# Moving the input's transposes behind the output's products in the second half of an attention period

## What is computed

```python
x = x + 0.5 * ffn(layernorm(x))        # ternary weights, exact gelu
x = x + attn(layernorm(x))             # rotary q and k, causal softmax
x = x + 0.5 * ffn(layernorm(x))

def attn(x):
    q, k, v = x @ Wq.T, x @ Wk.T, x @ Wv.T       # each [16, 256, 256], split in 16 heads
    q, k = rope(q), rope(k)
    scores = where(causal, q @ k.T / 4, -inf)
    return softmax(scores) @ v @ Wo.T
```

## Time and profile before

| | us |
|---|---|
| median of 3 runs (lowest, highest) | 606.04 (605.77, 607.61) |
| the profiled execution, its own time | 606.82 |
| its span, first to last instruction | 605.1 |
| PE busy in the span | 567.5 (94%) |
| DVE busy | 458.6 (76%) |
| ACT busy | 345.2 (57%) |
| attention stage, periods with both `XT` and `WO` (p = 1 to 11) | about 205 to 414 of the span |

### The profile page before, as it was taken

How to read it: one execution, slowest core, us unless ns; L and a number is a source line. 1 busy time by engine, 2 the same in 40 slices (tenths; PEclk the granted TensorE clock), 3 DMA queues, 4 the chain that set the end, 5 groups by cost and what they waited for, 6 DMA issues and landing times.

```text
span 605.1 us, 17855 instructions
## 1 busy us (share of the span) xinstructions
PE 567.5 (94%) x6596; PEld 497.1 (82%) x6596; DVE 458.6 (76%) x928; ACT 345.2 (57%) x610; POOL 229.8 (38%) x446
## 2 busy tenths in 40 slices
PE   1899999999689999999999999999878999999997
PEld 1789999999668888888888888888665788899996
DVE  5977777778687988879878798877572777777764
ACT  1765455556236666866667666576556655554542
POOL 6373333333646353542545435434131033333310
PEclk9999999999889999999999999999999999999999
DMA  6630000000867666655575555766500011111111
GB/s 204 213 111 6 0 0 0 0 0 4 242 181 207 184 188 187 166 149 174 165 200 166 149 165 159 206 165 168 153 2 3 1 36 35 35 35 35 35 35 36
DMA packets 71142, 63.45 MB, mean 105 GB/s; under 512 B 4130, under 2 KB 64322, under 8 KB 71106
## 3 DMA queue, kind: packets, MB, share of 16 engines
q1 hardware_dynamic: 69922, 62.81, 35.9%
q10 hardware_dynamic: 1184, 0.14, 0.2%
HBM read 33.03 MB, written 29.36 MB: 103 GB/s over the span
## 4 chain that ended last, share of the span: by engine, by line
PE 82%; DVE 9%; DMA 3%; ACT 2%; POOL 2%; issue 1%; SPq 1%; DVEq 0%; POOLq 0%
PE bank L173 18%; PE bank L534 17%; PE bank L1062 13%; PE bank L670 7%; PE bank L1057 6%; PE bank L1118 5%; PE bank L1193 4%; PE bank L1158 3%; PE bank L156 2%; PE bank L1121 2%; PE bank L1131 2%; DVE mx L860 2%; DVE g_lo L257 1%; DMA w1f<-w1t 1%; PE bank L1181 1%
## 5 line engine op out<-in xcount | busy, mean ns | idle before, releaser
L860 DVE TENSOR_REDUCE mx<-bank 128x2 f32<-128x512 f32 (+1 forms) x192 | 118.4, 681 | 32.8 <-PE bank L1062 32.7
L534 PE MATMUL bank<-w2q,g_hi 128*128 128x256 f32 x512 | 124.4, 284 | 1.8 <-DVE g_lo L257 1.5
L240 ACT ACTIVATE g<-bank,b1c 128x512 f32<-128x512 f32 x128 | 88.1, 691 | 64.7 <-PE bank L173 61.5
L534 PE MATMUL bank<-w2q,g_lo 128*128 128x256 f32 x512 | 122.5, 280 | 0.0
L982 ACT ACTIVATE probs<-bank 128x512 f32<-128x512 f32 x192 | 111.1, 597 | 11.7 <-PE bank L1062 4.1
L534 PEld LDWEIGHTS bank<-w2q,g_hi 128*128 128x128 f32 x512 | 96.4, 188 | 3.6 <-DVE w2q L372 1.3
L534 PEld LDWEIGHTS bank<-w2q,g_lo 128*128 128x128 f32 x512 | 96.4, 188 | 0.6
L312 POOL TENSOR_TENSOR res<-res,b2h 128x1024 f32 (+1 forms) x16 | 38.4, 2400 | 133.2 <-DVE xn L147 128.6
L257 DVE TENSOR_TENSOR g_lo<-g,g_hi 128x512 fp32r<-128x512 f32 x128 | 82.6, 686 | 3.1
L173 PE MATMUL bank<-xt_hi,w1q 128*128 128x512 f32 x240 | 76.9, 402 | 2.0 <-DVE xt_lo L167 2.0
L173 PE MATMUL bank<-xt_lo,w1q 128*128 128x512 f32 x240 | 76.1, 398 | 0.0
(11 more groups left out here) (129 smaller groups left out, 1172.6 us busy)
## 6 DMA issues: line engine op xcount, KB each, us to landing
qk_slots<-parts SPq DMA_DIRECT2D x32, 384.0 KB, 3.7
q<-qk_slots SPq DMA_DIRECT2D x32, 384.0 KB, 4.0
k<-qk_slots SPq DMA_DIRECT2D x32, 384.0 KB, 4.8
qk_slots<-parts SPq DMA_DIRECT2D x32, 256.0 KB, 3.4
res<-x SPq DMA_DIRECT2D x8, 512.0 KB, 3.6
qk_slots<-parts SPq DMA_DIRECT2D x32, 128.0 KB, 3.2
out<-res SPq DMA_DIRECT2D x8, 512.0 KB, 2.9
w1f<-w1t SPq DMA_DIRECT2D x2, 512.0 KB, 6.4
```

The source lines that it names most:

```text
L240: nc.scalar.activation(g[:, f, :], of[:], ACT.Gelu, bias=b1c[:, f:f + 1]).then_inc(g_ready, 1)
L534: last = nc.tensor.matmul(to[:, 0:D], part[:, f, t * P:(t + 1) * P], w2q[:, f, :], start=f == 0 and part is g_hi, stop=f == FC - 1 and par ...
L860: nc.vector.tensor_reduce(o, i, AX.X, ALU.max).then_inc(s_done, 1)
```

## The change

In a second half PE issues the twelve products of `WO` ahead of the four transposes of `XT`, and DVE issues `add_output` ahead of `low_xt`. Nothing else is changed, and every wait stays with its instruction.

```diff
@@ DVE, step(p, 1)
                     if p.has(0):
                         normed_heads(p, 1)
+                    if p.has(-1):
+                        add_output(p)
                     if p.has(4, 2):
                         low_xt(p)
-                    if p.has(-1):
-                        add_output(p)
@@ PE, step(p, 1)
                     if p.has(0):
                         OT(p, 1)
-                    if p.has(4, 2):
-                        XT(p)
                     if last:
                         hidden_ahead(pe, 5)
                         hidden_ahead(pe, 6)
                     if p.has(-1):
                         WO(p)
+                    if p.has(4, 2):
+                        XT(p)
```

## The result

The changed kernel takes 609.36 us in the median of 4 runs (608.78 to 610.11), the kernel before 606.25 us in the runs beside it (605.77 to 607.61): ratio 1.0048, 95% interval 1.0028 to 1.0068. The interval is clear of 1: by that ratio the change costs about 2.9 us, between 1.7 and 4.1; the two medians are 3.1 us apart. Two profiled executions can't give this by their spans alone (607.0 and 605.1 us, 1.9 apart), since the stretch ahead of the changed periods differs by itself from one execution to the next. The stretch from the `ANT` of period 1 to that of period 12, which holds all eleven changed periods, can.

A forecast was written before the change was run, and what follows sets the result against it. The prediction took PE to set the pace in the second halves; 2.58 us (periods 2, 4, 6, 8, 10, 11) plus 1.50 (five odd periods) gave 4.08, added to 606.04 for 610.1 us, range 607.8 to 612.6.

The forecast's parts named there:

- the likeliest case: Second halves: `WO` must wait for ACT's copy of the values, which `XT` used to fill; 609.6 to 611.1 us, chance 0.73.
- the sum: Periods 1 to 11: 2.58 us of even periods and period 11 plus 1.50 of odd ones, 4.08 us slower.
- rival 1: PE later in each period: the delay is absorbed, no change within 1.8 us; 606 to 607.9 us, chance 0.10.
- What bounds the place: Second half: PE's list is dense and PE sets the pace, so 0.1 us more on PE lengthens the period by 0.1.
- The even periods, 0.43: Periods 2, 4, 6, 8, 10 and 11: `WO` starts as before, `XT` delays `MT` by 0.43 us each, 2.58 us.
- The odd periods, 0.30: Five odd loop periods with statistics: old hole merges into the wait for the copy, `MT` 0.30 us later each, 1.50 us.
- The slot's details: PE, period 6: `WO` to the next piece 1.53 us, then `XT` takes a slot of 0.43 us ahead of `MT`.
- the bounds of 3.6 and 4.5: Total loss over the changed periods if the slot of `XT` takes 0.39 or 0.47 us instead of 0.43.
- DVE, nothing: DVE's reordering costs nothing, hidden in idle time ahead of the maxima, which shrinks from 1.34 to about 0.8 us.
- ACT, nothing: ACT's late copy of the transposed input costs nothing; it fits with 0.06 us to spare before the copy of the heads.
- POOL and SP, nothing: Second `low` comes late; `pad` ends about 294.35, before the split at 294.55; rows of maxima 0.4 us later; no cost.
- The clock: PE around the holes: no charge for slower products; a rival had it fall in second halves, about 626 us, chance 0.02.

## Why the prediction was right

The range held 609.36, the mechanism of the likeliest case is the one that came, and its size was a little over: 4.08 us in the sum, 3.84 in the trace, 2.9 (1.7 to 4.1) by the ratio of the runs. The median itself lies 0.2 us below the 609.6 to 611.1 that the forecast gave to this case, in the gap above rival 1; that it was this case and no absorbed delay is read from the traces, not from the median.

- *What bounds the place.* "A tenth of a microsecond more on PE is a tenth more in the period": shown for the second half, by the delayed copy. A wait 0.27 us longer gave 0.29 in each period of the changed kernel, and nothing where PE does not wait for the copy.
- *The even periods, 0.43.* Measured 0.41 in period 6, and 0.40 from its `ANT` to the next. `WO` started where it did, as period 12 had shown.
- *The odd periods, 0.30.* The period from 283.26 to 302.31 is 19.05 us; before it was 18.76: +0.29, and +0.28 in most others. The old hole was not saved, it was merged into the new one.
- *The slot's details.* From the start of `WO` to the next piece I took 1.53 us, the time to `MT`. To `XT` it is 306.60 - 305.17 = 1.43. Against this, from the start of `MT` to the next scores it is 308.77 - 307.02 = 1.75 us instead of 1.66. The two errors nearly cancel. One sign of the forecast did not come, though: `MT` is later behind `ANT` by 0.32 us in period 6 and by 0.20 in period 5, not by 0.43 and 0.30, and the last 0.1 us arises behind the start of `MT`. Why these two pieces take another time in the new order was not tried. The 3.84 us are below the sum by 11 x 0.02, and the bounds of 3.6 and 4.5 held.
- *DVE, nothing.* Shown by the two halves of the change, to within 0.15 us over the eleven periods.
- *ACT, nothing, "the thinnest cover".* It held. Measured from `ANT`'s first load, the copy of the transposed input started at 5.02 us, where I had 5.08, and the copy of the heads had 0.22 us of idle time ahead of it instead of 0.06.
- *POOL and SP, nothing.* The `pad` ends 293.94 - 283.26 = 10.68 us behind `ANT`, worked out as 10.72. On SP I expected the rows of maxima 0.4 us later, and they were not: 311.75 is 9.44 behind `ANT`, as before. The prediction had spaced the six issues evenly and so put the fourth at 309.43; in the row it starts at 309.05. It did go out late, at 309.83, but its issue took 0.37 us instead of 0.83, and that of the sixth 0.59 instead of 0.99, and the six together were as long as before. Why a late issue is a short one was not tried. The fourth store before, then after:

```profile
309.05 0.83 SPq L686 DMA_DIRECT2D qk_slots<-parts  x1
```

```profile
309.83 0.37 SPq L686 DMA_DIRECT2D qk_slots<-parts  x1
...
311.75 0.76 SPq L756 DMA_DIRECT2D q<-mt  x1
```

- *The clock.* The granted clock was 1.00 around the hole of 0.59 us in period 5, and 1.00 in the mean from period 1 to 12. The Trainium skill's rule that brief, frequent idle times of PE can make it swing between its clock levels ("TensorE: Matmul & The Clock Gate", section "A second HAM failure mode: psum-queue depth-cycling") did not come to bear on these eleven holes; the last section has a place where a longer wait is followed by a lower clock.

## What to carry to other kernels

Where an engine's list is dense and in order, ask of every piece what it covers: here 0.43 us of transposes were free because they stood inside another engine's copy, and the same work a few instructions later cost 0.40 to 0.42 us in the even periods and in period 11, nearly its whole length, and 0.28 in the odd ones, where an old hole was merged into the new. A period of the same trace that lacks the piece, such as the last ones of a pipeline, shows beforehand what the wait looks like without it. And when a piece waits for a buffer and its neighbour could use another that is free sooner, exchanging the buffers can remove the wait: here it did, at no instruction more.

## What was not expected of the hardware

The granted clock of PE differs between executions at places that no edit touches. In the first half of period 14 PE waits 1.33 us for POOL ahead of `MT` and then 0.68 or 0.69 more ahead of `PV`, in all ten profiled kernels. In the kernel with exchanged banks and late statistics, and in the same kernel with the delayed copy, the windows behind these waits read:

```profile
438.20:441.20 3.00, 2.76 (x34) 1.61 (x36) 0.70 (x3) 0.11 (x1) 2.03 (x6) 0.53 0.03 10
```

```profile
437.80:440.80 3.00, 2.83 (x66) 2.40 (x66) 0.71 (x4) 1.10 (x3) 1.95 (x6) 1.00 0.04 10
```

The first ran near the 1.2 GHz level, with half the products in the window, and from the `ANT` of period 13 to that of period 14 it took 445.30 - 426.79 = 18.51 us; the second stayed at 2.4 GHz and took 444.10 - 426.31 = 17.79. Of the ten profiled executions three fell there (the exchanged banks at 0.66, the same with late statistics, and the changed kernel with the delayed copy at 0.58); in the other seven it is 1.00 behind the same waits. In the stretch from 160 to 180 us, at the start of the attention stage, the mean granted clock was 0.83 in the kernel before and 0.91 after:

```profile
160.00:180.00 20.00, 14.36 (x163) 11.68 (x161) 15.14 (x30) 5.94 (x13) 8.25 (x14) 0.83 0.79 220
```

```profile
160.00:180.00 20.00, 14.59 (x194) 11.53 (x196) 16.43 (x32) 7.08 (x15) 9.90 (x18) 0.91 0.83 225
```

Period 1 was reached anywhere from 206.75 to 208.84 us in these executions. The times of single runs go with the clock: of the 20 runs of the kernel before beside the last experiments, the seven with a mean granted clock of 0.997 took 604.92 to 605.52 us and the four with 0.990 took 607.05 to 607.87. So the stretch from period 1 to 12, at 1.00 throughout, tells small costs apart that the medians do not. What decides whether the clock falls at such a wait was not tried.
